# Local layers of a four-layer stack: the MLP's last unit over all 128 rows, and the weighted values computed behind the scores into one bank

## The reference

```
def _layer(x, wqkv, qs, ksc, wo, lg, lb, w1, b1, w2, b2):
    b, n, _ = x.shape
    h = shift_token(x)                       # the second half of the columns comes from the token before
    qkv = h @ wqkv
    q, k, v = jnp.split(qkv, 3, axis=-1)     # 8 heads of 64
    ...
    q = l2norm(q) * qs
    k = l2norm(k) * ksc
    q, k = rotary_xpos(q, k)
    o = local_attention(q, k, v)             # causal softmax in a window of 128
    o = o.transpose(0, 2, 1, 3).reshape(b, n, INNER)
    x = x + o @ wo
    h = shift_token(x)
    mu = h.mean(-1, keepdims=True)
    var = h.var(-1, keepdims=True)
    h = (h - mu) / jnp.sqrt(var + 1e-05) * lg + lb
    h = h @ w1 + b1                          # 256 -> 2 * 682
    a, g = jnp.split(h, 2, axis=-1)
    h = a * jax.nn.gelu(g, approximate=False)
    x = x + h @ w2 + b2                      # 682 -> 256
    return x
...
x = x + jnp.tanh(g_ffn[1]) * _L1_ffn_ref(_layernorm(x, axis=-1), ...)
```

## Time and profile before

| | us |
|---|---|
| median of 3 runs | 1744.72 |
| lowest and highest run | 1743.67 and 1747.17 |
| span of the profiled execution | 1741.7 |
| TensorE busy | 1660.0 (95%) |
| DVE, ACT, POOL busy | 1117.6, 1000.9, 955.9 |

### The profile page before, as it was taken

How to read it: one execution, slowest core, us unless ns; L and a number is a source line. 1 busy time by engine, 2 the same in 40 slices (tenths; PEclk the granted TensorE clock), 3 DMA queues, 4 the chain that set the end, 5 groups by cost and what they waited for, 6 DMA issues and landing times. The chain is left out here.

```text
span 1741.7 us, 38448 instructions
## 1 busy us (share of the span) xinstructions
PE 1660.0 (95%) x11910; PEld 1293.1 (74%) x11910; DVE 1117.6 (64%) x3319; ACT 1000.9 (57%) x2824; POOL 955.9 (55%) x1182
## 2 busy tenths in 40 slices
PE   7999799989889999999999999999998999999998
PEld 4778488858547777777777777768876888867886
DVE  4787776637556666666667666547885353337875
ACT  4677455547436665666665666448782355537775
POOL 2356676558455566555555555333777244457762
PEclk9999999999999999999999999999999999999999
DMA  4333286565200000000000000013435345432200
GB/s 157 97 101 121 85 253 202 160 233 176 109 7 4 4 4 6 4 4 4 4 4 6 4 4 4 5 50 107 137 141 187 89 126 145 139 134 74 77 26 25
DMA packets 79668, 140.27 MB, mean 81 GB/s; under 512 B 11728, under 2 KB 61104, under 8 KB 77296
## 3 DMA queue, kind: packets, MB, share of 16 engines
q1 hardware_dynamic: 65744, 98.22, 18.1%
q0 software_dynamic: 13728, 39.60, 6.4%
HBM read 84.88 MB, written 50.82 MB: 78 GB/s over the span
## 5 line engine op out<-in xcount | busy, mean ns | idle before, releaser
L1596 POOL TENSOR_TENSOR L1f_rn<-L1f_ss,L1f_root_c 128x8 f32<-128x8 f32 x64 | 105.5, 1648 | 184.3 <-DVE L1f_ss L1899 181.8
L1732 PE MATMUL L1f_psQ<-L1f_xT,arena 128*128 128x128 f32 x1408 | 172.4, 275 | 0.9 <-ACT L1f_xT L1807 0.9
L1732 PEld LDWEIGHTS L1f_psQ<-L1f_xT,arena 128*128 128x128 f32 x1408 | 169.5, 192 | 4.4 <-ACT L1f_xT L1807 1.1
L1825 ACT ACTIVATE L1f_sg<-L1f_psQ,vec1f 128x128 f32<-128x128 f32 x192 | 63.4, 364 | 138.0 <-PE L1f_psQ L1732 136.8
L2125 POOL DMA_INDIRECT outs_L2f<-L2f_tiles_ys,L2f_tiles_spot x79 | 75.8, 960 | 119.5 <-ACT L2f_tiles_ys L2273 104.3
L1611 POOL TENSOR_TENSOR L1f_rot<-L1f_qn,L1f_sinT 128x512 f32<-128x512 f32 x64 | 113.0, 1786 | 29.0 <-DVE L1f_qn L1915 29.0
L1945 DVE SCALAR_TENSOR_TENSOR L1f_hid<-L1f_psQ,vec1f,L1f_sg 128x128 f32<-128x128 f32 x192 | 61.2, 346 | 90.1 <-ACT L1f_sg L1825 89.6
L1656 PE MATMUL L1f_psQ<-arena,L1f_hT 128*128 128x512 f32 x256 | 118.4, 605 | 0.6 <-ACT L1f_hT L1814 0.6
L1744 PE MATMUL L1f_psB<-arena,L1f_hid 128*128 128x256 f32 (+1 forms) x384 | 99.7, 388 | 0.0
L2125 POOL DMA_INDIRECT outs_L0f<-L0f_tiles_ys,L0f_tiles_spot x79 | 75.9, 961 | 43.0 <-ACT L0f_tiles_ys L2273 34.8
L1601 POOL TENSOR_TENSOR L1f_pr<-L1f_pr,L1f_rs 128x512 f32<-128x512 f32 x64 | 95.6, 1514 | 6.2 <-DVE L1f_rs L1909 6.2
(11 more groups left out here) (535 smaller groups left out, 4705.6 us busy)
## 6 DMA issues: line engine op xcount, KB each, us to landing
L0f_tiles_xs<-rows_L0f SPq DMA_DIRECT2D x79, 144.0 KB
L2f_tiles_xs<-rows_L2f SPq DMA_DIRECT2D x79, 144.0 KB, 2.2
arena<-in_w_L2f SPq DMA_DIRECT2D x8, 1120.0 KB, 5.8
arena<-in_w_L1f SPq DMA_DIRECT2D x8, 1088.0 KB, 7.3
L1x_got<-outs_L0f SPq DMA_DIRECT2D x16, 512.0 KB, 3.9
L3x_got<-outs_L2f SPq DMA_DIRECT2D x16, 512.0 KB, 3.3
arena<-in_w_L0f SPq DMA_DIRECT2D x8, 768.0 KB, 4.7
rows_L0f<-zero SPq DMA_DIRECT2D x31, 144.0 KB
```

Of the source, the lines that this page charges most:

```text
L1596: nc.gpsimd.tensor_tensor(rn[:, s.p, h], ss[:, s.p, h], root_c[:, 0:LH], ALU.pow).then_inc(s_rn, 1)
L1732: mm = nc.tensor.matmul(out, w, xT[:, k], start=(k == 0), stop=(k == KC - 1), skip_group_check=True)
L1825: nc.scalar.activation(sg[to, u], unit_out(u, 0, of), ACT.Gelu, bias=column(s, 2 * KC + u)[of]).then_inc(s_sg, 1)
```

## The change

Three things are changed, all in `local_layers`. First, the lower half of hid's last unit is cleared once at the start of the phase, and the last `down` matmul takes all 128 rows instead of 64 (the weights' lower half of that unit is zero too). Second, `values` is moved on TensorE from behind `values_in` to directly behind `scores`, its eight matmuls write into the first bank of psP, in one piece, and it signals once instead of twice; ACT copies that bank to oT with one copy of 512 columns instead of two of 256. `turn_hidden` and `turn_in` write into psP's second bank instead of psA. Third, DVE's copy of the turned weights stands ahead of `results` in the round instead of behind it. The waits follow the banks.

```
-            pool.wait_ge(s_one, 4)
+            nc.gpsimd.memset(hid[LOWER, U - 1], 0.0).then_inc(s_one, 1)
+            pool.wait_ge(s_one, 5)
...
             def scores(s):
                 pe.wait_ge(s_kT, s.n + 1)
-                after(pe, s_oT, 2 * s.n - 2)
...
             def values(s):
-                pe.wait_ge(s_exp, min(2 * s.n + 3, 2 * N))
                 pe.wait_ge(s_vx, s.n + 1)
-                after(pe, s_done, s.n - 1)
                 for k in range(4):
-                    to = psS[:, 0] if k < 2 else psB[:, :]
                     for r in range(2):
                         if k == 0:
                             pe.wait_ge(s_pT1 if r else s_pT0, s.n + 1)
                         h = 2 * k + r
-                        mm = nc.tensor.matmul(to[64 * r:64 * r + 64, (k % 2) * P:(k % 2 + 1) * P], v[:, s.n % 3, h * LD:(h + 1) * LD],
+                        mm = nc.tensor.matmul(psP[64 * r:64 * r + 64, 0, k * P:(k + 1) * P], v[:, s.n % 3, h * LD:(h + 1) * LD],
                                               pT[:, r, k * P:(k + 1) * P], start=True, stop=True, skip_group_check=True)
-                    if k % 2:
-                        mm.then_inc(s_pv, 1)
+                mm.then_inc(s_pv, 1)

             def values_in(s):
-                after(pe, s_ln, 2 * (s.n - 2))
+                after(pe, s_vx, s.n)
                 product(psA[:, :], s, 2, s_v)

             def output(s):
-                pe.wait_ge(s_oT, 2 * s.n + 2)
+                pe.wait_ge(s_oT, s.n + 1)
...
             def turn_hidden(s):
                 pe.wait_ge(s_ln, 2 * s.n + 2)
-                pe.wait_ge(s_vx, min(s.n + 4, N))
+                pe.wait_ge(s_pT1, min(s.n + 2, N))
                 for k in range(KC):
-                    mm = nc.tensor.transpose(psA[:, k * P:(k + 1) * P], hn[:, k * P:(k + 1) * P], c.ident)
+                    mm = nc.tensor.transpose(psP[:, 1, k * P:(k + 1) * P], hn[:, k * P:(k + 1) * P], c.ident)
...
             def turn_in(s):
-                after(pe, s_vx, s.n)
-                after(pe, s_ln, 2 * (s.n - 3))
+                after(pe, s_pT1, s.n - 2)
+                after(pe, s_kT, s.n - 1)
...
             def down(s, j):
-                    of = UPPER if u == U - 1 else slice(0, P)
-                    mm = nc.tensor.matmul(psB[:, 0:D], hid[of, u], part(s, UNITS_AT + u * UNIT_GLU + 2 * D, D)[of],
+                    mm = nc.tensor.matmul(psB[:, 0:D], hid[:, u], part(s, UNITS_AT + u * UNIT_GLU + 2 * D, D),
                                           start=(u == 0), stop=(u == U - 1), skip_group_check=True)
...
             def turn(s):
-                after(pe, s_pT0, s.n - 1)
-                after(pe, s_pT1, s.n - 1)
+                after(pe, s_oT, s.n - 1)
+                after(pe, s_xT, s.n - 2)
+                pe.wait_ge(s_hT, min(s.n + 2, N))
...
-            rounds([(turn_weights, -2), (scores, -1), (queries_keys, 0), (values_in, 0), (values, -2), (turn_hidden, -3),
+            rounds([(turn_weights, -2), (scores, -1), (values, -2), (queries_keys, 0), (values_in, 0), (turn_hidden, -3),
...
             def outputs(s):
                 after(act, s_out, s.n)
-                for i, of in enumerate((psS[:, 0], psB[:, :])):
-                    act.wait_ge(s_pv, 2 * s.n + i + 1)
-                    nc.scalar.activation(oT[:, 2 * i:2 * i + 2].rearrange("p k t -> p (k t)"), of[:, 0:2 * P], ACT.Copy).then_inc(s_oT, 1)
+                act.wait_ge(s_pv, s.n + 1)
+                nc.scalar.activation(oT[:, :].rearrange("p k t -> p (k t)"), psP[:, 0], ACT.Copy).then_inc(s_oT, 1)
...
-            rounds([(row_stats, 4), (results, -4), (turned_weights, -2), (at(tops, 0), -1), (at(tops, 1), -1), (at(squares, 0), 0),
+            rounds([(turned_weights, -2), (row_stats, 4), (results, -4), (at(tops, 0), -1), (at(tops, 1), -1), (at(squares, 0), 0),
```

More of the change, by code:

```diff
@@ L1626, in _ @@
             c.wait(pe, "L1f0")
-            pe.wait_ge(s_one, 3)
+            pe.wait_ge(s_one, 2)
             def scores(s):
@@ L1708, in turn_in @@
                     pe.wait_ge(s_done, s.n - NB + 1)
-                after(pe, s_vx, s.n)
-                after(pe, s_ln, 2 * (s.n - 3))
+                after(pe, s_pT1, s.n - 2)
+                after(pe, s_kT, s.n - 1)
                 for k in range(KC):
-                    mm = nc.tensor.transpose(psA[:, D + k * P:D + (k + 1) * P], Y[:, own(s), k * P:(k + 1) * P], c.ident)
+                    mm = nc.tensor.transpose(psP[:, 1, D + k * P:D + (k + 1) * P], Y[:, own(s), k * P:(k + 1) * P], c.ident)
                 mm.then_inc(s_T, 1)
@@ L1767, in _ @@
             c.wait(act, "L1f0")
-            act.wait_ge(s_one, 3)
+            act.wait_ge(s_one, 4)
             def exps(s, r):
@@ L1780, in turned_weights @@
                 act.wait_ge(s_pt, 2 * s.n + 1)
-                after(act, s_pv, 2 * s.n)
+                after(act, s_pv, s.n)
                 nc.scalar.activation(pT[:, 0], psP[:, 0], ACT.Copy).then_inc(s_pT0, 1)
@@ L1790, in outputs @@
                 after(act, s_out, s.n)
-                for i, of in enumerate((psS[:, 0], psB[:, :])):
-                    act.wait_ge(s_pv, 2 * s.n + i + 1)
-                    nc.scalar.activation(oT[:, 2 * i:2 * i + 2].rearrange("p k t -> p (k t)"), of[:, 0:2 * P], ACT.Copy).then_inc(s_oT, 1)
+                act.wait_ge(s_pv, s.n + 1)
+                nc.scalar.activation(oT[:, :].rearrange("p k t -> p (k t)"), psP[:, 0], ACT.Copy).then_inc(s_oT, 1)
             def values_in(s):
                 act.wait_ge(s_v, s.n + 1)
-                after(act, s_pv, 2 * (s.n - 2))
+                after(act, s_pv, s.n - 2)
                 nc.scalar.activation(v[:, s.n % 3], psA[:, :], ACT.Copy).then_inc(s_vx, 1)
@@ L1806, in affine @@
                 for k in range(KC):
-                    ins = nc.scalar.activation(xT[:, k], psA[:, k * P:(k + 1) * P], ACT.Identity, scale=column(s, k), bias=column(s, KC + k))
+                    ins = nc.scalar.activation(xT[:, k], psP[:, 1, k * P:(k + 1) * P], ACT.Identity, scale=column(s, k), bias=column(s, KC + k))
                 ins.then_inc(s_xT, 1)
@@ L1812, in rows @@
                 after(act, s_v, s.n - 1)
-                nc.scalar.activation(hT[:, s.p, 0], psA[:, D:D + P], ACT.Copy)
-                nc.scalar.activation(hT[:, s.p, 1, 1:P], psA[:, D + P:2 * D - 1], ACT.Copy).then_inc(s_hT, 1)
+                nc.scalar.activation(hT[:, s.p, 0], psP[:, 1, D:D + P], ACT.Copy)
+                nc.scalar.activation(hT[:, s.p, 1, 1:P], psP[:, 1, D + P:2 * D - 1], ACT.Copy).then_inc(s_hT, 1)
             def gelu_table(s):
@@ L1876, in turned_weights @@
                 dve.wait_ge(s_pt, 2 * s.n + 2)
-                after(dve, s_pv, 2 * s.n)
+                after(dve, s_pv, s.n)
                 nc.vector.tensor_copy(pT[:, 1], psP[:, 1]).then_inc(s_pT1, 1)
```

2 lines of the change are left out of this document (1 added, 1 removed).

## The result

The changed kernel takes 1758.06 us (median of 5 runs, 1757.53 to 1759.54), the kernel before 1743.8 in the runs beside it. The ratio is 1.0071, with a 95% interval of 1.0054 to 1.0088. The forecast was 1757.5 us, from a base of 1744.72.

The account below looks back on a forecast made before the run. TensorE's list was taken to bound each round, with ACT's oT copies just in time. A round's +1.03 − 0.32 − 0.27 = +0.44 us over 29 rounds gave +12.8, with the edges +12.9: forecast 1757.5 us, range 1747 to 1765.

Parts of the forecast that it names:

- What bounds it: Steady rounds: TensorE's own list sets 19.97 us, but ACT's copies to oT are just in time, with no slack.
- Values behind the scores, +1.03: TensorE's eight values matmuls now precede the queries: everything from L1656 starts 1.03 us later; values don't wait for pT.
- One copy behind v, −0.32: From values_in's last piece to the output product: 1.78 us instead of 2.10, with ACT's copy to oT behind v.
- the wait of 0.80: TensorE ahead of the output product: waits 0.80 us every round for ACT's copy to oT.
- The last unit, −0.27: down's last matmul over 128 rows: no change of shape, saving 0.27 us a round, bounds 0.28 and 0.19.
- The sum of a round, +0.44: Steady round of the local layers: +1.03 − 0.32 − 0.27 = +0.44 us, over 29 rounds +12.8.
- qr's chain, 0.18 us to spare: Queries through squares, norms and rotation to qr and L1754: starts 1.03 us later, 0.18 of 0.50 slack left, no wait.
- The first rounds, +0.71, and the last ones, −0.6: Round without MLP ahead of the 29: +0.71 us; at the end round 32's moved wait +0.4, rounds 32 to 34 −0.8, round 33 −0.2.
- A: Rival: TensorE's stops at shape changes decide and the wait is hidden; 12.6 us over 30 rounds, 1732 us; chance 0.10.
- B: Rival: the wait and the stops cancel, ACT's spacing and copy 0.4 us shorter together; 1744 to 1746 us; chance 0.07.
- C: Rival: the tops' delay makes qr's chain the bound, L1754 waits 0.3 us; round +0.74, time 1766 us; chance 0.10.
- D: Rival: each 0.8 us wait lowers TensorE's granted clock, costing 45 us over 30 rounds; time 1800 us; chance 0.02.

Follow-up runs that it names:

- e1: The changed kernel with ACT's copy to oT one place earlier in its list, ahead of the copy to v; ratio 1.0071, round 20.42 us.
- e7: The changed kernel with one of POOL's two rotation products cut to one head of eight, nothing else; ratio 1.0074, round 20.47 us.
- e8: The changed kernel with the values back behind values_in on TensorE, still in one piece into psP with one copy to oT; ratio 1.0001, round 20.01 us.
- e2: The kernel before with only the last down matmul over 128 rows and the memset; ratio 0.9969, round 19.74 us.
- e3: The changed kernel with the lines on down taken back, so the last unit over 64 rows again; ratio 1.0110, round 20.67 us.
- e9: The changed kernel with the first four transposes of L1651 waiting only for the copy to qT, the others for kT; ratio 1.0042, round 20.32 us.
- e10: The kernel of e5 with the last unit over 64 rows again; ratio to the kernel before 0.9906, round 19.70 us.
- e5: The changed kernel with queries and keys first in TensorE's round, ACT's and VectorE's lists reordered to follow; ratio to the kernel before 0.9854, round 19.31 us.
- e4: The changed kernel with the copy to oT as two of 256 columns from the same bank; ratio 1.0069, round 20.50 us.
- e6: The changed kernel with the copy to oT ahead of that to v and one POOL rotation product cut to one head; ratio 0.9909, round 19.49 us.

## Why the prediction was right

Point by point, by its own terms:

- **What bounds it.** Right. Full records hid a wait that was just in time, as the earlier trace rows showed, and this is where the change lost.
- **Values behind the scores, +1.03.** Measured 956.73 − 955.71 = 1.02. The copies to pT end at 954.29 + 0.69 = 954.98, 0.7 ahead of the values, as forecast.
- **One copy behind v, −0.32.** Measured 1.77 − 2.10 = −0.33. Of the wait of 0.80 the row shows 0.74; the two transposes ahead of it now start 0.22 us apart (in e1 as well), so by the starts it is 0.9 (963.33 against 962.21 + 0.22). e7 shows that it acts by itself, e8 that the place is its cause.
- **The last unit, −0.27.** Mis-sized: 953.19 − 951.37 = 1.82 against 2.02, −0.20, and −0.23 a round by e2 and by the changed kernel against e3. The prediction named the copy to kT as late next and let the transposes follow it by 0.05; here it ends at 953.05 and they start at 953.19, 0.14 behind. e9 takes this wait away and the unit gives 0.35, of which 0.06 are at the transposes. By this and e10 the cost of the two changes of shape is larger than the 0.28 that I read, since part of it lies in the piece behind.
- **The sum of a round, +0.44.** 1.02 − 0.33 − 0.20 = +0.49, less 0.02 from L1651 to the scores: 0.47, measured 20.44 − 19.97 = 0.47. The unit's error of 0.07 is partly offset by three of 0.01 to 0.02 on the other side, so 0.03 a round was missed, 0.8 us in 29. The terms were right, but the closeness of the time is in part luck: the forecast was a change of 12.8 us and the medians differ by 14.3, and 0.9 of this does not show since the kernel before came out at 1743.8 and not at the 1744.72 that the forecast started from.
- **qr's chain, 0.18 us to spare.** Right in that L1754 doesn't wait in a steady round (970.48, with qr done at 968.46 + 1.83 = 970.29), so 0.19. The prediction took the chain over whole; in fact qr starts 0.33 us earlier behind the queries than before and takes 0.30 longer; the last section shows why the one makes up for the other. What the prediction didn't draw from it, and my expectation of e1 neither, is that this chain was a second bound of the same size: with the values ahead of the queries the early copy to oT did not make the kernel any faster, e1 shows. In round 2, where no MLP stands between the output product and L1754, L1754 did wait for qr. VectorE in the steady round, and TensorE in round 2:

```profile
968.46 1.83 DVE L1932 TENSOR_TENSOR L1f_qr<-L1f_cosd,L1f_rot 128x1024 f32<-128x1024 f32 x1
```

```profile
515.04 1.99 PE L1689 MATMUL L1f_psB<-arena,L1f_oT 128*128 128x256 f32 x8 [0.96 <-ACT L1f_oT L1788]
...
522.08 1.09 PE L1754 MATMUL L1f_psP<-consts,L1f_qr 128*128 128x128 f32 x8 [0.29 <-DVE L1f_qr L1932]
```

- **The first rounds, +0.71, and the last ones, −0.6.** Measured +1.1 and −0.4. What the first has over the forecast is mostly that wait for qr, 0.29. In the last the moved wait is 2.46 us instead of 1.95, and the clock falls behind it again, now over 1123 to 1131 (0.79); L1689 takes 2.93 there.
- **The rivals.** A (stops decide, 1732) falls with the waits' row, though its mechanism is real: e5 has the same three changes of shape and no wait, and is faster. B falls. C's wait for qr comes new in round 2 alone, and not through the tops: L1754 comes 13.63 us behind the queries there in both kernels (522.08 − 508.45, and 519.13 − 505.50 before), so it moved with the queries. D falls: 29 waits of 0.8 us at a clock of 1.00.

The Trainium skill (TensorEngine Tiling (Array Packing), Key Properties) says that changing the tiling mode drains TensorE. e10 beside e5 agrees, with 0.39 us for the way into one narrow matmul and out of it.

## What to carry to other kernels

An operation that is moved on one engine has a consumer on another with a list of its own: read there behind what it will be taken up, because its result is not ready when it is computed but when that list comes to it. Before a wait is removed, work out the next one to the same precision; here two chains of 20.4 us lay over each other, and removing either alone gave nothing. And when work must be put ahead of something, ask what the longest chain through the round begins with, and put that first of all.

## What the runs showed that was not expected

VectorE's addition to qr (128x1024) took 1.53 us before, 1.83 in the changed kernel, 2.04 in e1 and 1.21 in e5, with the same operands; and POOL's two products of the scaling (128x512) took 3.02 in e1, where they run beside it, and 2.04 in e5, where they are done before it:

```profile
935.26 2.04 POOL L1602 TENSOR_TENSOR L1f_pr<-L1f_pr,L1f_rs 128x512 f32<-128x512 f32 x2
```

```profile
937.44 1.21 DVE L1932 TENSOR_TENSOR L1f_qr<-L1f_cosd,L1f_rot 128x1024 f32<-128x1024 f32 x1
```

So they slow each other when they overlap, by 0.8 and 1.0 us in e1, and the rows show in which way: the one that begins second gives way. POOL's first product of the two, by itself, and in e5 the first product of the rotation with VectorE's cosd (128x1024) behind it:

```profile
950.40 1.04 POOL L1602 TENSOR_TENSOR L1f_pr<-L1f_pr,L1f_rs 128x512 f32<-128x512 f32 x1
```

```profile
931.82 1.27 POOL L1612 TENSOR_TENSOR L1f_rot<-L1f_qn,L1f_sinT 128x512 f32<-128x512 f32 x1 [0.90 <-DVE L1f_qn L1910]
932.25 1.92 DVE L1925 TENSOR_TENSOR L1f_cosd<-L1f_qn,L1f_cosT 128x1024 f32<-128x1024 f32 x1
```

In e1 POOL's product begins at 950.40, 0.08 ahead of qr, and takes 1.04, its usual time; qr, begun at 950.48, ends at 952.52, 1.08 behind that product's end. In the kernel before, the changed kernel, e2, e3, e4, e6, e7 and e9, qr begins 0.2 to 0.6 behind the same product and again ends 1.08 behind its end, so the later it begins, the shorter it looks. In e8 it begins about 0.1 ahead, takes 1.25, and POOL's product takes 2.02. In e5 (and e10) cosd begins 0.43 behind POOL's product and takes 1.92, again to 1.08 behind its end; in the other runs it begins 0.05 ahead and takes 1.23, and the product takes 2.31 instead of 1.27. This is why qr in e1 started earlier and was done no earlier: POOL's scaling, which is no part of the chain to qr, stood ahead of it. Whether the scaling put behind qr would free e1's kernel was not run. A chain's length therefore can't be taken over unchanged when its pieces come to lie beside others; this is what e1's expectation missed at qr.

The copies of 256 columns, each 0.385 us by itself, take 0.65 for two in a row.

The clock can fall in one profile and not in the other at the same place: ahead of the stage, behind a wait of 0.90 us that both have, L1361 took 1.77 us in the changed kernel and 1.16 before, and L1370 1.91 instead of 1.03. The windows from 456 to 464 us show a mean granted clock of 0.79 and of 1.00:

```profile
458.08 1.77 PE L1361 MATMUL L1x_psH<-L1x_x1T,arena 128*128 128x128 f32 x8 [0.90 <-ACT L1x_x1T L1418]
459.64 1.91 PE L1370 MATMUL L1x_psO<-arena,L1x_h1T 128*128 128x256 f32 x4
```

```profile
456.00:464.00 8.00, 6.31 (x29) 5.30 (x31) 2.70 (x8) 2.73 (x7) 1.98 (x7) 0.79 0.01 2
456.00:464.00 8.00, 6.58 (x38) 4.78 (x39) 3.95 (x12) 2.60 (x7) 2.17 (x6) 1.00 0.01 2
```
